# Four chained residual layers in split fp32: the rows of the split operands and two small tensors change places in SBUF

## The reference

```python
x = x + L0(x)   # x @ (quantised(w0 + lora_delta) * scale + lora_delta).T
x = x + L1(x)   # x @ W.T + 2 * sum over experts of gate * (x @ A_e.T) @ B_e.T
x = x + L2(x)   # x @ W.T + b + 2 * (x @ lora_As[id]) @ lora_Bs[id]
x = x + L3(x)   # x @ weight[id].T, another matrix for each sequence
```

## Time and profile before

| | before |
|---|---|
| median of 3 executions | 649.85 us (649.56 to 649.92) |
| the profiled execution | 649.47 us |
| its span, first to last instruction | 647.7 us |
| TensorE, matmuls | 642.5 us (99%), 3992 records |
| TensorE, weight loads | 591.9 us (91%) |
| VectorE | 500.9 us (77%) |
| ScalarE | 365.0 us (56%) |
| GpSimd | 91.6 us (14%) |
| granted TensorE clock | 1.00 |
| DMA | 67.32 MB, mean 104 GB/s |

### The profile page before, as it was taken

One profiled execution on the slowest core, in us unless ns is written; L12 is line 12 of the kernel. 1 busy time (PEld: TensorE's weight loads), 2 busy tenths in 40 slices (PEclk: granted clock), 3 DMA queues, 4 the chain that ended last, 5 costly groups with the idle time before them and its releaser, 6 DMA issues.

```text
span 647.7 us, 10326 instructions
## 1 busy us (share of the span) xinstructions
PE 642.5 (99%) x3992; PEld 591.9 (91%) x3992; DVE 500.9 (77%) x645; ACT 365.0 (56%) x549; POOL 91.6 (14%) x120
## 2 busy tenths in 40 slices
PE   8999999999999999999999999999999999999997
PEld 8899989999999999998889999889999889999886
DVE  6899999879980539968886877888687889686753
ACT  6774573971821346646664745764645665654553
POOL 2320225004110010002230001222001221000010
PEclk9999999999999999999999999999999999999999
DMA  8772112111002002122672222674212575002472
GB/s 274 212 203 82 49 32 66 33 35 37 29 32 99 1 1 90 35 68 95 210 243 95 64 66 70 207 258 140 66 33 99 162 261 187 1 1 66 129 235 92
DMA packets 46020, 67.32 MB, mean 104 GB/s; under 512 B 3604, under 2 KB 32020, under 8 KB 45972
## 3 DMA queue, kind: packets, MB, share of 16 engines
q1 hardware_dynamic: 40900, 58.28, 28.7%
q10 hardware_dynamic: 5072, 8.39, 3.6%
HBM read 58.27 MB, written 8.39 MB: 103 GB/s over the span
## 4 chain that ended last, share of the span: by engine, by line
PE 99%; DVE 0%; POOL 0%; issue 0%; POOLq 0%
PE ps L1260 30%; PE ps L1262 30%; PE ps L1261 30%; PE ps L1403 4%; PE ps L1405 1%; PE ps L1271 1%; PE ps L1432 1%; PE ps L1356 1%; PE ps L1448 0%; PE ps L1458 0%; PE ps L1460 0%; PE ps L1440 0%; DVE tmp L1248 0%; DVE tmp L1250 0%; POOL ident L539 0%
## 5 line engine op out<-in xcount | busy, mean ns | idle before, releaser
L1260 PE MATMUL ps<-e_both,ring_hi 128*128 128x384 f32 (+3 forms) x384 | 133.6, 348 | 0.0
L1262 PE MATMUL ps<-e_both,ring_lo 128*128 128x384 f32 (+3 forms) x384 | 132.9, 346 | 0.0
L1261 PE MATMUL ps<-x_both,e_both 128*128 128x256 f32 x448 | 125.7, 281 | 0.0
L898 DVE TENSOR_TENSOR e_both<-raw,e_both 128x512 fp32r<-128x512 f32 x128 | 90.9, 732 | 30.0 <-ACT e_both L772 29.4
L1262 PE MATMUL ps<-e_both,e_mid 128*128 128x512 f32 (+2 forms) x288 | 110.1, 382 | 0.0
L1261 PE MATMUL ps<-e_both,e_mid 128*128 128x512 f32 (+2 forms) x288 | 109.9, 381 | 0.0
L1260 PE MATMUL ps<-e_both,e_mid 128*128 128x512 f32 (+2 forms) x288 | 109.8, 381 | 0.0
L772 ACT ACTIVATE e_both<-raw 128x512 fp32r<-128x512 f32 x128 | 78.9, 628 | 53.7 <-PE ps L1262 53.4
L588 POOL TENSOR_TENSOR raw<-raw,ident 128x128 f32<-128x128 f32 x64 | 45.3, 711 | 350.4 <-DMA raw<-w_t 350.4
L1261 PEld LDWEIGHTS ps<-x_both,e_both 128*128 128x128 f32 x448 | 84.7, 189 | 0.0
L1260 PEld LDWEIGHTS ps<-e_both,ring_hi 128*128 128x128 f32 x384 | 72.2, 188 | 5.7
(11 more groups left out here) (175 smaller groups left out, 1271.4 us busy)
## 6 DMA issues: line engine op xcount, KB each, us to landing
raw<-w_t SPq DMA_DIRECT2D x64, 512.0 KB, 4.2
w_w<-x_t SPq DMA_DIRECT2D x16, 512.0 KB, 3.7
w_w<-w SPq DMA_DIRECT2D x15, 512.0 KB, 5.2
y<-tmp ACTq DMA_DIRECT2D x30, 256.0 KB, 3.5
e_both_w<-w_t SPq DMA_DIRECT2D x5, 512.0 KB, 8.1
e_both_w<-w_t SPq DMA_DIRECT2D x4, 384.0 KB, 6.4
e_mid_w<-bs SPq DMA_DIRECT2D x24, 64.0 KB, 2.9
e_mid_w<-b_cat SPq DMA_DIRECT2D x4, 128.0 KB, 6.1
```

The lines of the kernel that those rows point to most:

```text
L898: return dve.tensor_tensor(out, whole, hi.bitcast(F32), ALU.subtract)
L1260: pe.matmul(out, a[0], b_[0], start=start, stop=False, **kw)
L1261: pe.matmul(out, a[0], b_[1], start=False, stop=False, **kw)
L1262: return pe.matmul(out, a[1], b_[0], start=False, stop=stop, **kw)
```

## The change

Four things about places, and nothing else:

- `e_both` becomes [P, KT, 2, EW]: high row k and low row k stand beside each other. The two are 5,248 bytes apart and not 41,984; neighbours in k are 10,496 bytes apart and not 5,248. The views `e_hi` and `e_lo` follow, and so does the access of L1403.
- `cbt`, 192 bytes, is declared between `e_mid` and `x_both`. All that comes from `x_both` to `bc_lo` lies 192 bytes further on.
- `ids_sb`, 64 bytes, is declared between `bc_lo` and `br_hi`. So `br_hi`, `br_lo`, `br_now`, `ident` and the next ones up to `scales` lie 256 bytes further on, which is 64 more than `bc_hi` and `bc_lo`.
- From `cbs` to `lbias`, behind the old place of `cbt`, it is 64 bytes; from `lg` on, behind the old place of `ids_sb`, nothing.

```diff
-            e_both_w = place("e_both_w", [P, 2, KT, EW])
+            e_both_w = place("e_both_w", [P, KT, 2, EW])
             mid_w = place("e_mid_w", [P, KT * ES])
+            place("cbt_w", [P, 6, NL])
             w0_w = place("w0_w", [P, KT, D])
...
-        e_both = sb("e_both", [P, 2, KT, EW], F32R)
+        e_both = sb("e_both", [P, KT, 2, EW], F32R)
         mid = sb("e_mid", [P, KT * ES], F32R)
+        cbt = sb("cbt", [P, 6, NL], F32)
         x_both = sb("x_both", [P, KT, D], F32R)
...
         bc_lo = sb("bc_lo", [P, D], F32R)
+        ids_sb = sb("ids_sb", [1, 2, NB], I32)
         br_hi = sb("br_hi", [P, A0], F32R)
...
-        cbt = sb("cbt", [P, 6, NL], F32)
...
-        ids_sb = sb("ids_sb", [1, 2, NB], I32)
...
-        e_hi, e_lo = e_both[:, 0, :, :], e_both[:, 1, :, :]
-        e_hi_w, e_lo_w = e_both_w[:, 0, :, :], e_both_w[:, 1, :, :]
+        e_hi, e_lo = e_both[:, :, 0, :], e_both[:, :, 1, :]
+        e_hi_w, e_lo_w = e_both_w[:, :, 0, :], e_both_w[:, :, 1, :]
...
-                                  e_both[:, :, k, ecols], start=k == 0, stop=False, skip_group_check=True)
+                                  e_both[:, k, :, ecols], start=k == 0, stop=False, skip_group_check=True)
```

## The result

| | before | changed |
|---|---|---|
| median | 649.74 us (5 runs, 649.42 to 649.92) | 643.1 us (5 runs, 642.85 to 643.43) |
| ratio | | 0.99, 95% interval 0.9889 to 0.991 |
| profiled execution | 649.47 us | 643.43 us |
| its span | 647.7 us | 641.6 us |

The change takes 6.6 us off the median, 1.0%, and 6.0 us off the profiled execution. I had forecast 2.8 us. The direction is right, the time lies in the range, and the size is less than half of what came.

A forecast was written before the change was run, and what follows sets the result against it. Matmul pace was taken to bound the kernel, TensorE waiting for no other engine after the start. Block products -1.1, y products -1.1, low rank -0.4, gates -0.2 sum to -2.8 us: 649.85 to 647.0 us, range 641.0 to 651.2.

The forecast's parts named there:

- What bounds it: Whole kernel: matmuls cover 642.5 of 647.7 us, TensorE waits only 1.6 us at the start; only matmul pace can change.
- Block products: 1344 matmuls of 256 columns: pace from 119.0 to 118.2 ns, -1.1 us, bounds -2.0 and +2.2 us.
- 28.3 us for 240: Sign that the forecast is right: 240 block-product matmuls in 28.3 us, about 118 ns each.
- the lower bound: Block products at the cheapest 256-column stretch in the trace, 117.5 ns, giving -2.0 us.
- y products: 768 y_product matmuls: odd ring slots become as the even ones, -1.1 us taken, between -2.6 and +1.3 us.
- Low rank: 128 pairs of L1403 and L1405 at 0.25 us: L1405's weight load may get quicker, -0.4 us, bounds -1.3 and +1.3.
- Phase 1 and gates: Phase 1 chunks: 0, bounds -1.4 to +1.4 us; 256 gates matmuls: -0.2 us, bounds -0.7 to +0.2.
- Nothing changes: Rival, 27%: addresses are indifferent to PE, the terms cancel, 649.85 us.
- Slower, weight loads dearer: Rival, 13%: weight loads set the block products' pace at 120.6 ns, +2.2 us; 651.5 us, 653.4 at most.
- Its limit: Slower rival's deciding pace: block products slower than 119.8 ns, said to use up the other terms.
- Much faster, the collision of load and stream goes away: Rival, 8%: reading 192 bytes apart frees block products and gates to 113 ns, saving 9.6 us; 638 us.
- Its objection: Argument against the much faster rival: the 64-byte distances of phase 1's step 1 free nothing.

The follow-up runs named there:

- e4_kick: Changed kernel with two identity transposes, output overwritten, ahead of block product 0 in each group; 639.46 us (0.9845), again 639.57 us (0.9844).
- e1_rows_only: Changed kernel with cbt and ids_sb back at their old places, so only the rows of e_both alternate; 648.40 us (0.9984).
- e2_x_only: Kernel before with only cbt moved ahead of x_both, so x and the rings lie 192 bytes further on; 641.40 us (0.9875).
- e3_no_ids: Changed kernel with ids_sb at its old place; 643.27 us (0.9903).
- f4_kick1: Changed kernel with one identity transpose, output overwritten, ahead of block product 0 in each group; 641.59 us (0.9875).
- f3_x192_ring: Kernel before with cbt moved ahead of x_both, and y_product's ring laid with high parts in even rows, low parts in odd; 643.90 us (0.9908).

## Why the prediction was right or wrong

- **What bounds it**: right. No stage of phase 2 gained a wait of TensorE; the gain came out of the pace of matmuls, by addresses alone. Only the short waits of the first 50 us, some 0.4 us, took a little of it back in the profiled execution.
- **Block products**: the first mis-sized term. I took -1.1 us, between stretches of 117.5 and 120.6 ns; they gave -3.1 us, under my bound of -2.0, and with x alone -7.2 us. Products 0 to 4 came at 117.9 ns, near the 118.2 that I took, and filled the sign "28.3 us for 240" to the digit. That was luck: e4_kick runs the same products at 113.3 ns. The miss is in products 5 and 6, -2.1 us where my pace gives -0.3. The failing step is the lower bound: I let the cheapest 256-column stretch stand as an end, though no such stretch had the distance that the change brings. The pace of 113.3 ns was in no row of the kernel before. The step behind it failed too: I read from the earlier trace rows that shifts of 64, 128 or 192 bytes cost and bring nothing. They are means over eight k and hide it. In step 0 of the kernel before, 256-column products take 119.3 to 119.7 ns a matmul for even k, where all stands at 0, and 116.0 to 116.3 for odd k, where the stream stands at 128 (from the starts in the chunk at 124.98). And in step 1 only every other low row stands at 64 or 192, so that chunk says little of a stage in which all of x does.
- **y products**: the second mis-sized term; the mechanism was right. I foresaw that odd slots would become like the even ones (-1.3 us) with -2.6 us as the bound for more, and took -1.1. It was -2.7: the first triple of each slot fell as well, from 231.8 to 226.7 ns. In the even slots it had been slow behind a slot at another place, while the quick triple of 0.68 us in the earlier trace rows is the one that follows a triple with the same places and stands at 0 itself. That was the hint. I also took 768 matmuls; by the code they are 792, since one in the last product is split in two, which changes nothing in the sum.
- **Low rank**: wrong in sign, -0.4 against +0.2 us, inside its bounds. e1_rows_only has +0.1, e2_x_only 0.0: the rows did it, together with x.
- **Phase 1 and gates**: 0 and -0.2 forecast, -0.5 and +0.1 measured. The step 0 stretches fell from 5.56 to 5.53 us and from 4.20 to 4.17. Over all of step 0, 117.5 us in the kernel before, it is -0.4 us with the short waits and -0.9 in e3_no_ids without them; e2_x_only has -1.0 there and e1_rows_only -0.1, so this is the shift of the rings.
- **The rivals.** "Nothing changes" falls: matmuls of one shape, with nothing to wait for, go at 233.3, 231.8 or 226.7 ns by their addresses alone. The page "SBUF — State Buffer" of the Trainium skill, section "Who interferes with whom", says that PE never waits on anyone. That is about other engines, and nothing here speaks against it: the pace is the same whether VectorE is busy 26.42 or 21.30 us of the stage. What failed is my step from it to addresses that are indifferent. "Slower, weight loads dearer" was half there: rows alone do make the block products 1.4 us slower, but x's shift outweighs it; that it is the weight loads was not shown. Its limit was worked out wrongly: 119.8 ns uses up 1.1 us, and the other terms were 1.7, which is 120.3 ns. "Much faster, the collision of load and stream goes away" had 8%, and was nearer in size: 113 ns was the pace that I named for it, and products 5 and 6 reached it. Whether load and stream collide, no run shows. Its objection, that step 1's distances free nothing, was the error above.

## What to carry to other kernels

Where TensorE never waits, look at the distance between starts, not at busy time, and compare the same shape in different stages: even differences of 1% are exact and repeat here, and they come from the places of the operands and from what ran just before. Try the parts of a layout change alone: here a 192-byte shift by itself (641.4 us) beat the whole change (643.1 us), and the whole change with two dummy transposes in each group beat both (639.5 us, 1.6% under the kernel before). Read the pace by k or by slot before calling an address harmless, since means over a chunk can hide it. And don't take the extremes of the trace as bounds for a case that the trace doesn't have.

## What was not expected of the hardware

- In the block products and `y_product`, where the places repeat in every product, the pace is steady to the ns and has few values. With 512 columns: 226.7 ns if high and low are streamed from the place at which the weights stand, 233.3 if the low parts are half a block off. With 256 columns: 113.3, 117.8 and 120.0 ns. The lowest of each is 17/16 of the columns' time at 2.4 GHz. Where the places alternate, as in the kernel before, the pace lies between such values (118.7 and 119.1 ns by k).
- The page "TensorE: Matmul & The Clock Gate" of the Trainium skill, section "Back-to-back issue gap", gives N/2.4 + 2.5 ns, which would be 215.8 ns for 512 columns. It calls that the gap of an isolated matmul, and has about 131 ns for a sustained stream with weight loads. The steady streams of 512 columns here don't go below 226.7 ns.
- Two of these paces exist for the same instructions and addresses (113.3 and 117.8 ns), the stream stays in one for at least 28 us, and the profile of f4_kick1 shows the choice flip between groups of one execution.
- Places repeat after some hundred bytes. x moved by 128 gives the time of the kernel before (649.82 against 649.75 us), x moved by 64 or 192 doesn't; with E's rows at 0 and 128 this can't tell a period of 128 bytes from one of 256. `y_product` can: a low part 128 bytes off costs 6.6 ns (f3_x192_ring), while the slots of the changed kernel, whose neighbours are 41 blocks of 256 bytes apart and so differ modulo 512, all go at 226.7. That fits a period of 256. What in the memory or the engine does it was not tested.
